# Narrow attention: in three beats of four the sums stand between the first scores of two row groups and those of the other two

## The reference

```python
def _L1_xattn_ref(q, k, v, Wq, bq, Wk, bk, Wv, bv, Wo, bo):
    qh = (q @ Wq + bq).reshape(B, LQ, HEADS, D_K).transpose(0, 2, 1, 3)
    kh = (k @ Wk + bk).reshape(B, LKV, HEADS, D_K).transpose(0, 2, 1, 3)
    vh = (v @ Wv + bv).reshape(B, LKV, HEADS, D_K).transpose(0, 2, 1, 3)
    scores = jnp.einsum('bhqd,bhkd->bhqk', qh, kh) * scale
    attn = jax.nn.softmax(scores, axis=-1)
    out = jnp.einsum('bhqk,bhkd->bhqd', attn, vh)
    concat = out.transpose(0, 2, 1, 3).reshape(B, LQ, D_MODEL)
    return concat @ Wo + bo
...
    x = _layernorm(x + _L1_xattn_ref(x, ctx_512, ctx_512, ...), axis=-1)
```

## Time and profile before

| | |
|---|---|
| median of 3 runs | 3566.37 us (3561.52 to 3566.6) |
| profiled execution | 3561.62 us |
| its span | 3559.8 us |
| mean granted TensorE clock over the span | 0.953 |
| busy share of the span: PE, PEld, DVE, ACT, POOL | 88%, 55%, 68%, 56%, 58% |
| narrow attention, first scores to last weighted sums | 2918.4 to 3313 us of the span |

### The profile page before, as it was taken

The page is one execution under the profiler, slowest core; times in us unless marked ns, Lnnn a source line. Parts: engine busy times, 40 slices in busy tenths (PEclk is TensorE's granted clock), DMA queues, the critical chain, the costliest instruction groups (busy, mean ns, idle before and its releaser), DMA issues. The chain is left out here.

```text
span 3559.8 us, 101883 instructions
## 1 busy us (share of the span) xinstructions
PE 3143.7 (88%) x41041; PEld 1946.3 (55%) x41041; DVE 2404.4 (68%) x5635; ACT 1981.7 (56%) x3574; POOL 2062.4 (58%) x1842
## 2 busy tenths in 40 slices
PE   6888788877899999898999998999999989999676
PEld 3433343333555555565666666675555545656575
DVE  5998999985555555485556555876777765666465
ACT  5666666663566666442555554335666646666354
POOL 5888888884678787663111113546777752433365
PEclk8999999988999999998999999999999989999798
DMA  4222222224700000000000000000000000000364
GB/s 145 98 88 90 91 91 88 90 87 160 259 2 2 2 2 2 16 1 12 5 5 5 5 2 6 1 8 8 2 2 2 2 17 17 27 16 15 94 173 118
DMA packets 50328, 165.43 MB, mean 46 GB/s; under 512 B 11822, under 2 KB 23217, under 8 KB 40784
## 3 DMA queue, kind: packets, MB, share of 16 engines
q1 hardware_dynamic: 45520, 150.43, 12.9%
q0 software_dynamic: 4352, 8.47, 0.7%
HBM read 149.89 MB, written 43.65 MB: 54 GB/s over the span
## 5 line engine op out<-in xcount | busy, mean ns | idle before, releaser
L529 DVE TENSOR_TENSOR_SCAN XC<-ssm_dA,ssm_db 128x2048 f32<-128x2048 f32 x128 | 565.2, 4415 | 69.8 <-PE ssm_db L374 59.9
L478 ACT ACTIVATE ssm_dA<-ssm_delta,ssm_nega 128x508 f32<-128x508 f32 x512 | 325.7, 707 | 139.4 <-DVE XC L529 136.2
L1219 POOL TENSOR_TENSOR self_pm<-self_pT,weights 128x512 f32<-128x512 f32 x256 | 322.7, 1294 | 61.7 <-ACT self_pT L948 60.2
L593 POOL TENSOR_TENSOR XC<-XC,XB 128x1536 f32<-128x1536 f32 x64 | 253.3, 3958 | 92.6 <-DVE XC L529 92.6
L374 PE MATMUL ssm_db<-XB,ssm_dxT 32*128 32x128 f32 x4096 | 166.8, 305 | 144.6 <-DVE XC L529 135.5
L1225 POOL TENSOR_TENSOR XC<-XC,XB 128x128 f32<-128x128 f32 x128 | 58.5, 457 | 400.5 <-DVE XB L1102 400.5
L593 POOL TENSOR_TENSOR ssm_hC<-XC,XB 128x1536 f32<-128x1536 f32 x64 | 256.2, 4003 | 54.7 <-DVE XC L529 54.6
L374 PEld LDWEIGHTS ssm_db<-XB,ssm_dxT 32*128 32x128 f32 x4096 | 140.0, 204 | 235.2 <-DVE XC L529 214.5
L1088 DVE TENSOR_REDUCE self_nmax<-self_scores 128x4 f32<-128x512 f32 x256 | 158.4, 681 | 87.2 <-PE self_scores L828 87.1
L2654 POOL TENSOR_TENSOR XC<-XC,weights 128x512 f32<-128x512 f32 x128 | 161.6, 1283 | 95.8 <-ACT XC L2488 95.8
L2662 POOL TENSOR_TENSOR XC<-XC,weights 128x512 f32<-128x512 f32 x128 | 161.3, 1281 | 34.5 <-ACT XC L2497 34.3
(11 more groups left out here) (456 smaller groups left out, 8375.6 us busy)
## 6 DMA issues: line engine op xcount, KB each, us to landing
XB<-c_rows SPq DMA_DIRECT2D x64, 1024.0 KB
sorted<-in_padding SPq DMA_DIRECT2D x1, 33280.0 KB, 109.0
experts_we<-in_w_experts SPq DMA_DIRECT2D x72, 323.0 KB, 3.5
experts_rt<-sorted SPq DMA_DIRECT2D x72, 65.0 KB
ssm_xT<-in_xT SPq DMA_DIRECT2D x16, 256.0 KB
XC<-in_w_experts SPq DMA_DIRECT2D x9, 256.0 KB
weights<-in_w_self SPq DMA_DIRECT2D x1, 1412.0 KB, 7.3
cross_ctx_t<-in_ctx SPq DMA_DIRECT2D x16, 77.0 KB
```

The costliest lines, as they stand in the source:

```text
L478: o = act.activation(dA[:, p % 2, :].rearrange("p (b k t) -> p b k t", b=GROUP, k=4)[:, :, k, 1:T], by_batch(delta[:, slot, half, :])[:, : ...
L529: dve.tensor_tensor_scan(states(p).rearrange("p m t -> p (m t)"), dA[:, p % 2, :], db[:, :], 0.0, ALU.mult, ALU.add).then_inc(h_ready, 1)
L593: pool.tensor_tensor(weighted(p).rearrange("p (b k) t -> p b k t", k=4)[:, :, 0:3, :], states(p).rearrange("p (b k) t -> p b k t", k=4)[:, ...
L1219: pool.tensor_tensor(pm[:, n % 2, r, :].rearrange("p (h t) -> p h t", h=4), pT[:, n % 2, r, :].rearrange("p (h t) -> p h t", h=4), bcast(V ...
```

## The change

`first_scores` takes the pair of row groups as an argument and is called twice. In the beats with t mod 4 other than 3 the sums stand between the two calls; in beat 3 they stand ahead of both, as before. The waits are the same ones, and the wait for `own_keys` (and, for the first batch of a group, `by_act`) stands ahead of each pair. 45 beats have sums between two pairs: t = 4 to 62 without every fourth.

```diff
--- before.py
+++ after.py
@@ -1410,21 +1410,20 @@
                                        wv[half(h), :])
                 mm.then_inc(proj_mm, 1)
 
-            def first_scores(n):
+            def first_scores(n, two):
                 s, b = n // GROUP % 2, n % GROUP
                 if b == 0:
                     pe.wait_ge(by_act, (n // GROUP + 1) * N_ACT)
                 pe.wait_ge(own_keys, n + 1)
-                for two in range(2):
-                    if n >= 3:
-                        pe.wait_ge(exp_ready, 4 * (n - 3) + 2 * two + 2)
-                    elif n:
-                        pe.wait_ge(max_ready, 4 * (n - 1) + 2 * two + 2)
-                    for r in (2 * two, 2 * two + 1):
-                        rows = slice(32 * r, 32 * r + 32)
-                        mm = pe.matmul(sc[r][:, 0:4 * TK].rearrange("p (j t) -> p j t", j=4), qa[rows, s, b * T:(b + 1) * T],
-                                       km[rows, s, b])
-                    mm.then_inc(s1_mm, 1)
+                if n >= 3:
+                    pe.wait_ge(exp_ready, 4 * (n - 3) + 2 * two + 2)
+                elif n:
+                    pe.wait_ge(max_ready, 4 * (n - 1) + 2 * two + 2)
+                for r in (2 * two, 2 * two + 1):
+                    rows = slice(32 * r, 32 * r + 32)
+                    mm = pe.matmul(sc[r][:, 0:4 * TK].rearrange("p (j t) -> p j t", j=4), qa[rows, s, b * T:(b + 1) * T],
+                                   km[rows, s, b])
+                mm.then_inc(s1_mm, 1)
 
             def turn(n):
                 pe.wait_ge(split_ready, 2 * (n + 1))
@@ -1528,10 +1527,15 @@
                     counts(g)
                 if g := comes(t, 2):
                     context(g)
-                if there(t - 3):
+                between = t % GROUP != 3
+                if there(t - 3) and not between:
                     sums(t - 3)
                 if there(t + 1):
-                    first_scores(t + 1)
+                    first_scores(t + 1, 0)
+                if there(t - 3) and between:
+                    sums(t - 3)
+                if there(t + 1):
+                    first_scores(t + 1, 1)
                 if there(t - 3):
                     weighted(t - 3)
                 if there(t):
```

## The result

| | before | changed |
|---|---|---|
| median of 5 runs | 3566.6 us (3561.52 to 3575.28) | 3598.56 us (3591.01 to 3602.84) |
| profiled execution, its span | 3561.62, 3559.8 us | 3602.84, 3601.0 us |
| mean granted clock over the span | 0.953 | 0.948 |
| narrow phase, from the first load of first scores to the last of weighted sums | 394.8 us | 430.3 us |

The ratio is 1.0088, with an interval of 1.0074 to 1.0102. The change makes the kernel some 32 us slower, where 12 were forecast, and outside the range. The direction was right; the size was not. The profiled executions lie 41 us apart: the changed one is the slowest of its five. Of these 41 us, 34.8 lie in the narrow phase, from its first turn to its last, and 4.8 ahead of it, in phases that the change doesn't touch.

A forecast was written before the change was run, and what follows sets the result against it. TensorE's queue was taken to set the pace. Added 32.0 us, less 28.4 saved, plus 8.7 of longer waits made 12.3 us slower; put on the before median of 3566.37 us, the forecast was 3578.5 us, range 3563 to 3587.

The forecast's parts named there:

- The stall goes: TensorE's second scores stop waiting for VectorE's maxima, 0.67 us a beat; 28.4 us saved over 45 beats.
- Half a stretch costs 0.71 us: First scores on two row groups take as long as on four; 45 beats get 0.71 us more, 32.0 us.
- Rival C: At each first half, half a stretch costs less than a whole, so not slower: 3563 or 3556 us; chance 0.09.
- the drain alone: Each added half costs only the tiling-mode drain, 0.20 us, 9 us over 45 beats in place of 32.0.
- D: The fourth row group's two weight loads run beneath the sums: 7 us back, +6 us, 3572; chance 0.04.
- ScalarE holds context: Later sums in beat 1 delay ScalarE's `qa`, so TensorE stands 0.50 us at context in 14 groups.
- No instruction is added except a repeat of one wait already met: The split of first scores in 45 beats adds only a repeated wait, with no time counted for it.
- Beat 2: Its first half waits 0.12 us more for an exponential; with the stand at context 14 x 0.62 = 8.7 us.
- four doubts about waits: Apparently the rivals: ScalarE not holding context (0.15), cheaper half stretch (0.09), loads running ahead (0.04), maxima staying late (0.11).

The follow-up runs named there:

- the filler: The changed kernel with one identity matmul by 512 columns, its product unused, ahead of the first half in beats 60, 61 and 62: 3592.78 us, ratio 1.0084.
- with one wait: The changed kernel without the repeated waits for own_keys and by_act ahead of the second pair of row groups: 3589.52 us, ratio 1.008.
- the last version above: The kernel before with two maxima in place of four and, in beat 0, all first scores ahead of the sums: 3555.41 us, ratio 0.9978.

## Why the prediction was wrong, point by point

**The stall goes: right.** The waits for maxima fell from 89 to 5, and from second scores to projection it is 1.23 us, as forecast.

**Half a stretch costs 0.71 us: right.** It measured 0.71 to 0.75 in every profile (0.75 behind context). Rival C, in which it costs less, is out, and so is the drain alone (0.20 us). The rule that a change of tiling mode drains TensorE (the Trainium skill, TensorEngine Tiling (Array Packing), Key Properties) agrees with the 0.20 and 0.42 us idle ahead of each stretch's loads, but not every switch here shows such a gap: the row-grouped load of the second scores follows that of the turn (128x128) after 0.06 us. It doesn't give the price of the stretch. D is out as well: the second half's loads stood 0.20 us idle behind the sums and the half took its full 0.72 us, so the fourth row group's loads brought nothing. They stand in the queue behind those of the third, which the sums use, so no run tests loads that could go ahead at once.

**ScalarE holds context: right.** It measured 0.54 us, 0.96 less 0.42, where 0.50 was forecast. With beat 1 unsplit it was gone, and with beat 0 unsplit it was the same 0.54.

**"No instruction is added except a repeat of one wait already met": too cheap.** The repeated wait costs 0.09 us a group, all of it in beat 3, where the second half waits for an exponential. Without it the group is 25.40 us and not 25.49, and with it alone, in the order of before, 24.64 and not 24.55.

**Beat 2: sized too small.** The other 0.1 us between the forecast's 25.29 and 25.49 is there: context is held 0.54 us and not 0.50, the first half of beat 2 starts 1.10 us behind context and not 1.05, and takes 0.75 us and not 0.71. With the repeated wait, 14 groups make 2.8 us. The other 1.5 us between 12.3 and 16.6 are spread over the phase, and I can't place them.

**The step that failed is one that the sum doesn't have.** It took all durations from rows at clock 1.00 and held the clock for given, a term put at nothing without a reason. With 16.6 us added to the median of before, 3566.37, the time would be 3583 by this estimate, inside the range; what took it out is the clock. Between beats 8 and 56, seven executions with beat 0 split (the change twice, and the runs with beats 12 to 55, with beats 0 and 2, with the filler, with one wait, and from 12 on) had 11 falls: 1, 2, 0, 3, 1, 2 and 2. Each began in beat 0, between turn 4k - 1 and turn 4k. Six executions without beat 0 split had none, one of them with groups as long as the change's (25.46 us). One fall of 6.8 us costs 3.1 us (turn 39 to 41 took 16.28 us in the change's first profile, and 13.17 in groups without a fall). At the end, five of six executions with halves and no filler had falls of 6.8 to 34 us in all, none of the six without halves there had one, and a row of fillers held the clock in the one execution that had them. The clock's share of the 35 us in the first profile is 18 us: 3.2 between beats 12 and 56, 1.4 from 56 to 60, 10.1 from 60 to 63, and 3.5 at the start, though the start isn't safely the change's (below).

That the falls come from the added halves is shown by the runs with and without beat 0, and with and without halves at the end. All 17 falls between beats 8 and 63 began 1.8 to 2.8 us behind the loads of a beat's first half, that is in its second half or in the weighted sums behind it. The row scores aren't needed for it in the last beats: four of the six falls there began in beats 61 and 62, which have none. In the second profile of the change the clock fell at 3319.3, in beat 61:

```profile
3317.08 0.33 PEld L1424 LDWEIGHTS narrow_scores<-XB,narrow_qa 32*128 32x128 f32 x4 [0.61 <-issue]
3317.82 0.81 PEld L1461 LDWEIGHTS narrow_sums<-narrow_pT,narrow_ones 77*32 77x32 f32 x32 [0.42 <-issue]
3318.83 0.30 PEld L1424 LDWEIGHTS narrow_scores<-XB,narrow_qa 32*128 32x128 f32 x4 [0.20 <-issue]
3319.73 1.48 PEld L1473 LDWEIGHTS narrow_out<-narrow_pT,narrow_v 77*32 77x32 f32 x32 [0.60 <-issue]
```

These beats also lack queries and context, and in steady groups beats 1 and 2 had no fall with the same halves, so a half alone isn't enough. That it is the idle row groups, and not the longer chain of short stretches as such, is my reading of what stands there; no run separates the two. The run with the whole first scores in that place, one stretch and no halves, had no fall, which speaks for it.

**What stays open is the start.** From turn 0 to 4 it took 20.4 to 23.2 us in six executions and 25.4 to 30.6 in seven. Of the long ones one has no halves anywhere near (25.4, the run split in beats 12 to 55), and another is the last version above, 26.0 us. So a late clock doesn't need the halves; what makes it late isn't shown. Where halves stand in beats 4 to 6 it stayed low past beat 4 in three of the five executions in which it was late; in the two late ones without such halves it didn't. Whether the halves hold it down there can't be said from so few.

**The range** took in four doubts about waits and 4 us for the scatter, and no doubt about the clock. Each of my rivals moved work between queues; none changed what TensorE is granted.

## What to carry to other kernels

Splitting a stretch of row-grouped matmuls can cost the stretch a second time: here two row groups took 0.71 us and all four 0.73. To give the next engine a head start, move the whole stretch, or shorten that engine's own work, as two reductions in place of four did here. On an engine that is busy the whole time, a reordering can still change the granted clock: where it strings together matmuls that fill only part of the array, compare the granted clock of the stretch, and count the clock among the rivals. When sums that another engine's long queue waits for are moved later, follow that queue to its last reader before counting the gain.

## What the runs showed of the hardware that I had not expected

- The granted clock fell to the 1.2 GHz level while TensorE was busy for 3.50 of 3.50 us ahead of one fall, and ahead of the 11 falls between beats 8 and 56 no gap between its loads was over 0.8 us. What stood just ahead of each were the row scores of 8 columns, two row groups of first scores (0.71 us), the sums (1.01 us) and the other two row groups.
- A met wait ahead of a late one costs 0.07 us: from the exponential's end to the load 0.12 us with it, 0.05 without.
- A VectorE maximum over two banks (128x616) takes 0.80 us and the pair 1.50, against 1.63 for four of one bank: 0.13 us less. That is as expected from two sizes of one bank elsewhere in the kernel before: 467 ns for the cross attention's 128x308 and 681 for the self attention's 128x512 (the expectation has both as the cross attention's).
